# A fused attention and FFN block on one core: score products from a stacked copy, or directly from the split queries and keys

## What is computed

```python
h = layernorm(x) * (1 + ca) + sa                     # modulated by c; sa, ca, ga, sb, cb, gb from silu(c) @ wmod
q = h @ Wq; k, v = split(h @ Wkv)                    # 16 heads of 64 channels
s = (q * 64**-0.5) @ k.T                             # 256 x 256 per head
p = where(causal_mask, 0, exp(s - max(s)))           # the maximum is over all keys, masked ones too
x = x + ga * (p @ v / (sum(p) + 1e-8) @ Wo + bo)
h = layernorm(x) * (1 + cb) + sb
x = x + gb * down(silu(gate(h)) * up(h))             # inputs and weights of the three rounded to FP4 in blocks of 16
```

## Time and profile before

| | us |
|---|---|
| median of 3 runs | 1399.65 |
| lowest, highest | 1399.06, 1401.82 |
| the profiled execution | 1400.84 |
| its span, from the first to the last instruction | 1399.0 |

### The profile page before, as it was taken

One profiled execution on the slowest core, in us unless ns is written; L12 is line 12 of the kernel. 1 busy time (PEld: TensorE's weight loads), 2 busy tenths in 40 slices (PEclk: granted clock), 3 DMA queues, 4 the chain that ended last, 5 costly groups with the idle time before them and its releaser, 6 DMA issues.

```text
span 1399.0 us, 37184 instructions
## 1 busy us (share of the span) xinstructions
PE 1322.9 (95%) x10194; PEld 1101.7 (79%) x10194; DVE 1145.8 (82%) x2821; ACT 960.9 (69%) x3269; POOL 866.3 (62%) x1582
## 2 busy tenths in 40 slices
PE   4899999999999999999999999999999999999993
PEld 2678888888887888888888888888888888888872
DVE  5678888888888888888888888888888888988874
ACT  2767677677667677767767767767776867777750
POOL 0546566676666766666666666666666666666663
PEclk9999999999999999999999999999999999999995
DMA  5767777777677767677777677766767776777730
GB/s 146 185 154 169 172 183 168 166 168 166 162 175 177 170 165 167 163 170 182 167 167 168 163 168 178 173 166 167 165 163 170 183 170 165 168 163 170 178 90 10
DMA packets 160941, 227.99 MB, mean 163 GB/s; under 512 B 27376, under 2 KB 90736, under 8 KB 160912
## 3 DMA queue, kind: packets, MB, share of 16 engines
q1 hardware_dynamic: 160912, 227.65, 68.6%
HBM read 21.94 MB, written 4.28 MB: 19 GB/s over the span
## 4 chain that ended last, share of the span: by engine, by line
DVE 45%; PE 33%; issue 12%; ACT 5%; SPq 2%; POOL 1%; DVEq 1%; DMA 1%; ACTq 0%; POOLq 0%
DVE neg_max L774 11%; PE ps_m L825 11%; PE ps_o L961 6%; PE ps_s L908 6%; DVE qk_parts L664 5%; PE ps_m L888 3%; DVE qy L61 3%; DVE amax L53 3%; DVE qm L65 3%; PE ps_s L917 3%; PE ps_t L804 3%; ACT probs L583 3%; DVE qm L64 3%; DVE xn L747 2%; DVE h_r L599 2%
## 5 line engine op out<-in xcount | busy, mean ns | idle before, releaser
L774 DVE TENSOR_REDUCE neg_max<-ps_s 128x2 f32<-128x512 f32 x512 | 349.7, 683 | 152.2 <-PE ps_s L908 145.3
L583 ACT ACTIVATE probs<-ps_s,neg_max 128x128 f32<-128x128 f32 (+1 forms) x1024 | 418.7, 428 | 25.4 <-PE ps_s L917 25.2
L456 POOL TENSOR_SCALAR probs<-probs,r_den 128x256 f32<-128x256 f32 (+1 forms) x768 | 379.0, 509 | 0.0
L454 POOL TENSOR_TENSOR probs<-probs,r_den 128x128 f32<-128x128 f32 x256 | 102.2, 399 | 410.7 <-DVE r_den L791 406.0
L908 PE MATMUL ps_s<-stack 128*128 128x256 f32 x2048 | 333.7, 289 | 4.1 <-DMA stack<-qk_parts 3.5
L908 PEld LDWEIGHTS ps_s<-stack 128*128 128x128 f32 x2048 | 286.2, 190 | 13.8 <-DMA stack<-qk_parts 4.5
L804 PE MATMUL ps_t<-ident,probs 128*128 128x128 f32 x1536 | 223.6, 276 | 7.8 <-POOL probs L456 7.5
L961 PE MATMUL ps_o<-probs_t,v 128*64 128x256 f32 (+1 forms) x2048 | 223.0, 339 | 0.1
L583 ACT ACTIVATION_READ_ACCUMULATOR probs<-ps_s,neg_max 128x1 f32 x1024 | 218.7, 214 | 0.0
L570 ACT COPY probs_t<-ps_t 128x384 f32<-128x384 f32 x160 | 76.7, 479 | 188.5 <-PE ps_t L804 188.5
L804 PEld LDWEIGHTS ps_t<-ident,probs 128*128 128x128 f32 x1536 | 172.4, 140 | 22.3 <-POOL probs L456 22.0
(11 more groups left out here) (109 smaller groups left out, 1960.0 us busy)
## 6 DMA issues: line engine op xcount, KB each, us to landing
stack<-qk_parts SPq DMA_DIRECT2D x512, 192.0 KB, 2.7
stack<-qk_parts SPq DMA_DIRECT2D x512, 128.0 KB, 2.7
stack<-qk_parts SPq DMA_DIRECT2D x512, 64.0 KB, 2.3
mod_a<-mod_rows SPq DMA_DIRECT2D x32, 256.0 KB, 3.8
x_in<-L_attn_x SPq DMA_DIRECT2D x32, 128.0 KB, 2.2
x_res<-L_attn_x SPq DMA_DIRECT2D x32, 128.0 KB, 2.2
out<-y_out SPq DMA_DIRECT2D x32, 128.0 KB, 1.9
mod_b<-mod_rows SPq DMA_DIRECT2D x32, 64.0 KB, 2.9
```

The costliest lines, as they stand in the source:

```text
L456: ins = nc.gpsimd.tensor_scalar(cols, cols, r_den[:, par, s:s + 1], 1.0, ALU.mult, ALU.mult)
L583: ins = nc.scalar.activation(probs[:, u % 4, h, t * P:(1 + 2 * t) * P], ps_s[:, scores_bank(u, h), t * N:t * N + (1 + t) * P], ACT.Exp, bi ...
L774: nc.vector.tensor_reduce(neg_max[:, par, 2 * h:2 * h + 2], ps_s[:, scores_bank(u, h), :].rearrange("p (t j) -> p t j", t=2), AX.X, ALU.ma ...
```

## The change

The stacked copy, its DMAs and its semaphores go. ACT and DVE write the parts of queries and keys to qk_r, which keeps four units, and the scores are computed from it: for each head and tile three products of 64 rows (low by high, high by low, high by high), twelve in a unit. The first head's operands lie on partitions 0 to 63 and the second's on 64 to 127, and the program alternates between them. ps_s has four banks, two for each of two units in turn, ps_t has one bank, and DVE takes the four maxima of a unit in one reduction.

PE's order in a unit becomes: scores, values, three transposes, a, three transposes, b, first mask, c, second mask. DVE's readers of a, b and c stand together after the reciprocals and the copy. ACT copies the outputs of the values first in a unit (in unit 3 it does so between its exponentials, after wo has been read), then the first transposes, a's high part, the second transposes. PLACES is written anew, and wo and down are cut in two steps of half the size. The norms' scaling uses scalar_tensor_tensor in place of tensor_scalar, h_r[0] is written by ACT, and some steps of DVE, POOL and SP stand a unit later.

```diff
-        qk_parts = sb("qk_parts", [P, 2, 2, 2, N], F32R)
-        stack = sb("stack", [P, 4, 2, 3, N], F32R)
+        qk_r = sb("qk_r", [P, 4, 2, 2, N], F32R)
...
-        ps_s = ctx.enter_context(nc.psum_tensor("ps_s", [P, 3, 512], F32))
-        ps_t = ctx.enter_context(nc.psum_tensor("ps_t", [P, 2, 512], F32))
+        ps_s = ctx.enter_context(nc.psum_tensor("ps_s", [P, 4, 512], F32))
+        ps_t = ctx.enter_context(nc.psum_tensor("ps_t", [P, 512], F32))
-        def scores_bank(u, h):
-
-            return u % 2 if h == 0 else 2
...
-        PT0_ON_ACT = (0, 1, 2, 3, 5)
+        PT0_ON_ACT = (1, 2, 3, 4, 6)
+        OT_LATE = (3,)
...
-            (0, "b"): ("xqt", 2, 0), (0, "c"): ("v", 0, 1), (1, "b"): ("gate", 2, 0), (1, "c"): ("up", 2, 0),
-            (2, "b"): ("gate", 2, 1), (2, "c"): ("up", 2, 1), (3, "b"): ("wo", 1, 0), (3, "c"): ("v", 0, 2),
-            (4, "b"): ("v", 0, 3), (4, "c"): ("xt", -1, 0), (5, "b"): ("hqt", 2, 0), (5, "c"): ("hqt", 2, 1),
-            (6, "c"): ("down", 2, 0), (7, "b"): ("v", -1, 0)}
+            (0, "b"): ("v", 0, 1), (0, "c"): ("xqt", 2, 0), (1, "b"): ("gate", 2, 0), (1, "c"): ("up", 2, 0),
+            (2, "b"): ("gate", 2, 1), (2, "c"): ("wo", 1, 0), (3, "b"): ("wo", 1, 1), (3, "c"): ("up", 2, 1),
+            (4, "b"): ("v", 0, 2), (4, "c"): ("v", 0, 3), (5, "b"): ("xt", -1, 0), (5, "c"): ("hqt", 2, 0),
+            (6, "b"): ("hqt", 2, 1), (6, "c"): ("v", -1, 0), (7, "b"): ("down", 2, 0), (7, "c"): ("down", 2, 1)}
...
-            def stack_unit(b, u):
...
-                    sp.dma_start(bottom[:, :, :], src[:, 1:4, :]).then_inc(done, 16)
-                    sp.dma_start(top[:, 1:3, :], src[:, 2:4, :]).then_inc(done, 16)
-                    sp.dma_start(top[:, 0, :], src[:, 0, :]).then_inc(done, 16)
...
+                    if u == 0 and has.prev2:
+
+                        if not isinstance(i, int) or i > 2:
+                            pool.wait_ge(y_ready, 2 * (i - 2))
+                        pool.wait_ge(wo_scaled, 2 * (i - 1))
+                        nc.gpsimd.tensor_tensor(x1_keep[:, :, :], attn[:, :, :], x_gb[:, :, :], ALU.add).then_inc(kept, 1)
...
+                            nc.scalar.copy(qk_r[:, k % 4, 0, :, :], ps_m[bank][:, :].rearrange("p (n j) -> p n j", n=2)
...
+                            for h in (h_t, h_r[0]):
+                                nc.scalar.activation(h[:, :], ps_m[bank][:, 0:N], ACT.Identity,
+                                                     bias=mod_t[:, 0, bass.ds(b, 1)],
+                                                     scale=mod_t[:, 1, bass.ds(b, 1)]).then_inc(ht_ready, 1)
...
+                    if has.unit(u - 3) and u not in OT_LATE:
+                        out_copy()
+                    if has.unit(u - 2) and u in PT0_ON_ACT:
+                        act.wait_ge(pt_full, 16 * i + 2 * (u - 2) + 1)
+                        nc.scalar.copy(probs_t[:, u % 2, 0, :], ps_t[:, 0:3 * P]).then_inc(pt0_ready, 1)
+                    shared_reads(u, "a")
+                    if has.unit(u - 2):
+                        act.wait_ge(pt_full, 16 * i + 2 * (u - 2) + 2)
+                        nc.scalar.copy(probs_t[:, u % 2, 1, :], ps_t[:, 0:3 * P]).then_inc(pt1_ready, 1)
+                    shared_reads(u, "b")
+                    if has.attn:
+                        exponentials(0)
+                    shared_reads(u, "c")
+                    if has.unit(u - 3) and u in OT_LATE:
+                        if has.prev:
+                            act.wait_ge(wo_full, 2 * i)
+                        out_copy()
+                    if has.attn:
+                        exponentials(1)
...
+                        nc.vector.tensor_tensor(attn[:, k, :], ps_m[bank][:, 0:P], mod_a[:, 0, :], ALU.mult).then_inc(wo_scaled, 1)
+                        dve.wait_ge(wo_scaled, 2 * b + k + 1)
                         dve.wait_ge(xgb_ready, b + 1)
-                        nc.vector.tensor_tensor(x1[:, :, :], attn[:, :, :], x_gb[:, :, :], ALU.add).then_inc(x1_steps, 1)
...
+                def normalized(dst, src, mv, r, ready):
+
+                    for t in range(2):
+                        nc.vector.scalar_tensor_tensor(dst[t], src[:, t, :], mv[:, t, 0:1], r[:, t:t + 1].to_broadcast([P, P]),
+                                                       ALU.subtract, ALU.mult).then_inc(ready, 1)
...
-                        for h in range(2):
-                            dve.wait_ge(s_full, 16 * i + 2 * u + h + 1)
-                            nc.vector.tensor_reduce(neg_max[:, par, 2 * h:2 * h + 2],
-                                                    ps_s[:, scores_bank(u, h), :].rearrange("p (t j) -> p t j", t=2),
-                                                    AX.X, ALU.max, negate=True).then_inc(max_ready, 1)
-                            if h == 0:
-                                shared_reads(u, "a")
-                    else:
-                        shared_reads(u, "a")
-                    if u == 5 and has.next:
-
-                        dve.wait_ge(ht_ready, i + 2)
-                        split(Steps(dve, hr_ready, 2, i + 1), h_t[:, :], [w[:, :] for w in h_r])
+                        dve.wait_ge(s_full, UNITS * i + u + 1)
+                        nc.vector.tensor_reduce(neg_max[:, par, :],
+                                                ps_s[:, 2 * par:2 * par + 2, :].rearrange("p b (t j) -> p (b t) j", t=2),
+                                                AX.X, ALU.max, negate=True).then_inc(max_ready, 1)
...
-                    shared_reads(u, "b")
                     if has.unit(u - 2) and u not in PT0_ON_ACT:
                         dve.wait_ge(pt_full, 16 * i + 2 * (u - 2) + 1)
-                        nc.vector.tensor_copy(probs_t[:, u % 2, 0, :], ps_t[:, 0, 0:3 * P]).then_inc(pt0_ready, 1)
+                        nc.vector.tensor_copy(probs_t[:, u % 2, 0, :], ps_t[:, 0:3 * P]).then_inc(pt0_ready, 1)
+                    shared_reads(u, "a")
+                    shared_reads(u, "b")
...
-                def scores(u, h):
+                def scores(u):
+                    pe.wait_ge(qk_ready, UNITS * i + u + 1)
+                    if has.after(u - 2):
+                        pe.wait_ge(exp_done, 16 * i + 2 * (u - 2) + 2)
+                    if i_is(i, 0) and u == 1:
+                        pe.wait_ge(setup_dve, SETUP_ROWS)
                     for t in range(2):
-                        for part in range(2):
-                            mm = nc.tensor.matmul(ps_s[:, scores_bank(u, h), t * N:(t + 1) * N],
-                                                  stack[:, u % 4, h, 0, t * P:(t + 1) * P], stack[:, u % 4, h, 2 - part, :],
-                                                  start=(t == 0 and part == 0), stop=(part == 1), skip_group_check=True)
+                        for n, (left, right) in enumerate(((0, 1), (1, 0), (0, 0))):
+                            for h in range(2):
+                                rows = slice(h * DH, (h + 1) * DH)
+                                mm = nc.tensor.matmul(ps_s[:, 2 * (u % 2) + h, t * N:(t + 1) * N],
+                                                      qk_r[rows, u % 4, left, 0, t * P:(t + 1) * P],
+                                                      qk_r[rows, u % 4, right, 1, :],
+                                                      start=(t == 0 and n == 0), stop=(n == 2), skip_group_check=True)
                     mm.then_inc(s_full, 1)
...
-                    pe.wait_ge(max_ready, 16 * i + 2 * u + h + 1)
-                    diagonals = ps_s[:, scores_bank(u, h), :].rearrange("p (n j) -> p n j", j=P)[:, 0:4:3, :]
+                    pe.wait_ge(max_ready, UNITS * i + u + 1)
+                    diagonals = ps_s[:, 2 * (u % 2) + h, :].rearrange("p (n j) -> p n j", j=P)[:, 0:4:3, :]
...
+                def probs_transposed(u, h):
+                    pe.wait_ge(probs_ready, 16 * i + 2 * (u - 2) + h + 1)
+                    if h == 1:
+                        pe.wait_ge(pt0_ready, UNITS * i + u - 1)
+                    elif has.after(u - 3):
+                        pe.wait_ge(pt1_ready, UNITS * i + u - 2)
+                    for c in range(3):
+                        mm = transpose(ps_t[:, c * P:(c + 1) * P], probs[:, (u - 2) % 4, h, c * P:(c + 1) * P])
+                    mm.then_inc(pt_full, 1)
...
                 for u in range(UNITS):
-                    par = u % 2
+                    if has.attn:
+                        scores(u)
+                    if has.unit(u - 3):
+                        values(u)
+                    if has.unit(u - 2):
+                        probs_transposed(u, 0)
                     at_place(u, "a")
-
-                    if has.attn:
-                        pe.wait_ge(stacked[par], STACKED * i + UNIT_STACKED * (u // 2 + 1))
-                        scores(u, 0)
+                    if has.unit(u - 2):
+                        probs_transposed(u, 1)
                     at_place(u, "b")
```

(16 more changed lines are left out.)

182 lines of the change are left out of this document (72 added, 110 removed).

## The result

| | before | after |
|---|---|---|
| median, us | 1399.82 (1399.06 to 1401.82) | 1501.70 (1500.00 to 1502.18) |
| ratio to before | | 1.0724, 95% interval 1.0707 to 1.0741 |
| profiled execution, its span | 1400.84, 1399.0 | 1501.62, 1499.7 |
| a steady batch | 41.46 | 44.70 |

The account below looks back on a forecast made before the run. PE was taken as the bound, with 2.4 us of stalls a batch. Seven units of 4.70 + c and unit 3 at 5.69 made 43.43 us against 41.46: +61 over 31 batches, -4 at the start, 1457 us, range 1385 to 1510.

Parts of the forecast that it names:

- PE's stream: PE's own steps in a unit without b and c: 3.46 us against 3.55 before, with qk at 0.71.
- rivals 1 (cheaper tiles): Entering row tiles, their first load and the step to column tiles cost nothing: 2.5 us a batch less, 1380; chance 0.16.
- 2 (rows not shared): The two heads' score products run one after another on PE: +0.71 us a unit, 1633; chance 0.07.
- 3 (loads not ahead): Weights are not loaded ahead within a row tile, five pairs more pay 0.11: +0.55 us a unit, 1593; chance 0.06.
- The wait that takes its place: c waits for a's read-out, 1.57 us from a's end on PE, starting 4.38 after the first score, in seven units.
- The waits for the maximum: Masks' 1.6 us of waits a batch go to nothing; one reduction of 1.2 us replaces two of 683 ns.
- Only unit 3, whose b is half of wo (1.75), stays on 3.46 + b + c: Unit 3 alone has no wait at c: 5.69 us; the other seven take 4.70 + c.
- Rival 4: DVE is late at qk's subtraction by 0.2 us in every unit, above all 2 and 6: 1507; chance 0.09.
- Unit 7: 5.36 us (4.70 + c, c being 0.66); DVE's late copy of the first transposes is swallowed by c's wait.
- one of the signs that I named for being wrong: PE waits at the second transposes for longer than 0.5 us, so the copy of the first ones sets the pace.
- The -4 at the start: Removing the stacking DMAs, which hold PE for 3.5 us of the span, gives -4 us once, nothing a batch.
- The clock: The chip halves PE's clock because PE waits in each unit; given no chance of its own.

Follow-up runs that it names:

- e2_between_first: The changed kernel with DVE's work of between(2), the rounding's first steps and the normalization, put ahead of unit 2's reader of c: 1470.42 us.
- the last two kernels here: Kernel with early place a and ScalarE's copies, its two left waits taken out: 1400.21 us; that one with normalization and GpSimd's rounding also moved: 1394.14 us.

## Why the prediction was right or wrong

- **PE's stream: right on the row tiles, 0.17 a unit short on qk.** The block of the scores was put at 0.82 + 0.10 and is 0.90 with 0.20 behind the mask; the values are 0.80 (predicted 0.80), the first transposes 0.30 (0.38). The row tiles pair up as the column tiles do, so rivals 1 (cheaper tiles), 2 (rows not shared) and 3 (loads not ahead) are out. But qk takes 0.44 + 0.46, and I had 0.71: its first weights still cost 0.08 and those of the second transposes behind it 0.11. In six units the wait at c covers this; unit 3 of e2_between_first, where PE waits for nothing, shows it, 5.86 for the 5.69 of the sum. Rival 3 was what the rule of the Trainium skill, "TensorE: Matmul & The Clock Gate", Part 3, would make of it, by which a weight load runs beside products only on other rows of the array; twelve products in 0.90 with loads of 187 ns leave no room for a bare load a pair, so the trace speaks against the rule here too. With the heads apart the last three products are all on the second head's rows and start 0.11 and 0.12 apart (748.08 and 748.20 behind 747.97), with loads of 184 ns.
- **The wait that takes its place: right in six units.** c was to start 4.38 after the first score; it does. The chain was right by itself (0.03 + 0.62 + 0.75 for 0.04 + 0.62 + 0.74); that the start of the chain fits to 0.01 as well is partly luck, for the transposes in front of it are 0.08 shorter and qk's first half 0.08 longer than put. Units 1, 2, 4, 5, 6 and 0 come within 0.06 of the numbers, and the copy done twice is passed on one for one in them. The prediction named seven units with a wait at c and unit 3 without: unit 7 has none, and unit 3 has the longest.
- **The waits for the maximum: right** for seven units: none is left there, and the one reduction takes 1.21 (1.2). The sentence said that they go to nothing "even where DVE is a whole microsecond late". In unit 3 it is 2.9 late, and the mask waits 0.14.
- **"Only unit 3, whose b is half of wo (1.75), stays on 3.46 + b + c": this step failed.** Unit 3 is 6.88, not 5.69: 1.19 a batch, 31 x 1.19 = 37 us of the 45. I gave every unit a DVE that is 0.6 late at most. Between units 2 and 3 it has 3.5 us of work, behind a reader that waits for c of unit 2, which this very change makes late. Rival 4 (DVE late at the subtraction) named the mechanism and between(2) with it, but spread it as 0.2 over all units; it is 1.2 in one. Moving that work ahead of the reader gives the 5.86 that the step had expected, 5.69, but for the 0.17 of qk.
- **Unit 7: 0.15 short.** DVE's copy of the first transposes is late by 0.53 at the second ones; I had it swallowed by the wait at c, and it is c's wait that is gone there. A wait of over 0.5 at this place was one of the signs that I named for being wrong, and for this unit it is. 0.15 x 31 = 5 us.
- **The -4 at the start: not there in the sum.** 31 x 3.24 = 100.4 leaves nothing of the difference of the spans, 100.7, for it. The first wo does start earlier, at 83.0 us against 84.6, but what follows the last one is 1.7 longer (41.9 and 40.2).
- **The clock:** 1.00 in the batch, and no part of the result, as put.

The sum by its own steps: 43.43 + 1.19 + 0.15 - 0.07 (the other units) = 44.70 a batch.

## What to carry to other kernels

A shared buffer has a turn-around: count, for each pair of steps that use one bank in turn, what lies between them on the engine that fills it against the time its reader takes; 1.57 us of reading behind 0.44 + b us of work made six of eight units wait, and with unit 3 mended this kernel was still 2.2 us a batch behind (43.64 and 41.46); no view of the busy time shows it before the change is made. Then follow the slowest reader through the work that stands between its steps, unit by unit: an engine with 24% idle time was 2.9 us late at one place of eight, and a mean hides that. When a step moves forward on the engine that writes, move its reader with it, and expect a wait that goes to come back at the next bound: the last two kernels here were to take away 1.1 and 1.0 us of waits a batch, and the batch fell by 0.24 and 0.16.

## What the hardware showed

- Products of 64 rows by 256 columns in float32r run side by side on the two halves of the array if they are neighbours in the stream: 0.90 us for twelve, with all that it costs to leave them. Six and six apart are 1.25, more than the pairs and less than one after another: three of the twelve start beside another one.
- Entering the row tiles costs 0.17 us (0.20 behind a mask, where a product over all rows with 256 columns stands at 0.03). The column tiles start 0.21 behind the last product in front, behind row tiles or full ones alike, of which the product's own time is 0.12.
- A 128x128 DVE operation from SBUF to SBUF took 983 ns beside POOL's rounding (tensor_tensor on 128x352) and 515 to 541 ns beside its scaling of probabilities, with the same instruction, and 346 ns with POOL idle; in the form that the kernel before has, 972 beside the rounding and 498 away from it. What ran on the other engine went with the difference, and the form did not. Why they hold each other up wasn't tried.
